# Scores for the maximum in PSUM banks of their own, one job ahead, and one bank for layer matmuls until the last exponential

## What is computed

```python
x_norm = _ln(x, norm1_w) * (1 + sc_msa) + sh_msa
q, k, v = ...                                   # projections, rotary embedding in layer 0
s = jnp.einsum('bqhd,bkhd->bhqk', q, k) * scale
s = jnp.where(mask, s, jnp.finfo(s.dtype).min)
a = jax.nn.softmax(s, axis=-1)
self_out = jnp.einsum('bhqk,bkhd->bqhd', a, v).reshape(b, s, d) @ attn_out_W
x = x + g_msa * self_out
h = jax.nn.gelu(xm @ mlp_W1 + mlp_b1, approximate=True)
x = x + g_mlp * (h @ mlp_W2 + mlp_b2)
```

## Time and profile before

| | us |
|---|---|
| median of 3 executions | 800.41 |
| lowest, highest | 796.43, 803.18 |
| the profiled execution | 800.15 |
| its span, first to last instruction | 798.3 |
| TensorE matmul busy | 648.6 (81%) |
| VectorE busy | 431.4 (54%) |
| ScalarE busy | 419.8 (53%) |
| GpSimd busy | 220.0 (28%) |
| mean granted clock of TensorE | 0.944 |

### The profile page before, as it was taken

The page is one execution under the profiler, slowest core; times in us unless marked ns, Lnnn a source line. Parts: engine busy times, 40 slices in busy tenths (PEclk is TensorE's granted clock), DMA queues, the critical chain, the costliest instruction groups (busy, mean ns, idle before and its releaser), DMA issues.

```text
span 798.3 us, 16559 instructions
## 1 busy us (share of the span) xinstructions
PE 648.6 (81%) x6694; PEld 364.3 (46%) x6732; DVE 431.4 (54%) x1121; ACT 419.8 (53%) x714; POOL 220.0 (28%) x319
## 2 busy tenths in 40 slices
PE   5579887888879987888788878888899788868887
PEld 5234443444444544445345444543456443644445
DVE  2447767646665676566655666666555652231222
ACT  0141634555465464736474457365676639465453
POOL 3142433305341434323431334143131420000000
PEclk9689999998989999999999899999999989989899
DMA  8500000000000000000000000000000000000000
GB/s 302 175 2 1 16 1 15 14 2 28 15 1 2 15 14 15 2 14 15 16 1 2 24 5 2 15 1 15 1 2 14 2 1 2 0 14 1 0 14 13
DMA packets 15314, 15.81 MB, mean 20 GB/s; under 512 B 1833, under 2 KB 13108, under 8 KB 14856
## 3 DMA queue, kind: packets, MB, share of 16 engines
q1 hardware_dynamic: 14572, 10.72, 4.5%
q10 hardware_dynamic: 668, 4.05, 1.3%
HBM read 13.66 MB, written 1.09 MB: 18 GB/s over the span
## 4 chain that ended last, share of the span: by engine, by line
PE 51%; ACT 27%; DVE 15%; issue 4%; POOL 1%; DMA 1%; SPq 0%; DVEq 0%; ACTq 0%; POOLq 0%
ACT P L576 13%; PE lin L938 12%; PE lin L951 9%; PE big L1027 8%; PE avp L1055 6%; DVE mhl L773 5%; PE big L1006 3%; ACT hT L559 3%; ACT xn L548 2%; PE big L1034 2%; DVE bst L725 2%; PE big L1022 2%; ACT hid L610 2%; PE lin L960 2%; DVE oT L805 1%
## 5 line engine op out<-in xcount | busy, mean ns | idle before, releaser
L773 DVE TENSOR_REDUCE mhl<-big 128x8 bf16<-128x616 f32 (+1 forms) x160 | 151.0, 963 | 95.0 <-PE big L1006 92.6
L504 POOL TENSOR_TENSOR qm<-qT,hm 128x512 f32<-128x512 f32 x80 | 88.0, 1100 | 125.8 <-ACT qT L541 77.3
L938 PE MATMUL lin<-hT,W 128*128 128x512 f32 x184 | 107.7, 673 | 14.5 <-ACT hid L610 6.1
L576 ACT ACTIVATE P<-big,padcol 128x1024 f32<-128x1024 f32 x64 | 67.9, 1114 | 73.0 <-PE big L1034 73.0
L576 ACT ACTIVATE P<-big 128x1024 f32<-128x1024 f32 x64 | 62.0, 1021 | 78.0 <-PE big L1034 77.9
L1027 PE MATMUL big<-qm,kT 32*128 32x512 f32 x640 | 99.7, 695 | 0.0
L467 POOL TENSOR_SCALAR rstd<-mv 128x4 f32<-128x4 f32 (+1 forms) x36 | 8.4, 233 | 313.7 <-DVE mv L731 313.5
L1055 PE MATMUL avp<-P,Vp 128*32 128x128 f32 x2560 | 91.0, 285 | 1.3 <-DVE Vp L740 1.2
L490 POOL TENSOR_TENSOR kbm<-kT,hm 128x308 bf16<-128x308 f32 (+1 forms) x80 | 68.2, 853 | 58.0 <-PE big L1006 47.9
L1055 PEld LDWEIGHTS avp<-P,Vp 128*32 128x32 f32 x2560 | 68.2, 113 | 29.0 <-issue 24.5
L1006 PE MATMUL big<-kbm,qb 32*128 32x308 bf16 (+1 forms) x320 | 54.6, 342 | 29.0 <-ACT P L576 27.5
(11 more groups left out here) (160 smaller groups left out, 929.7 us busy)
## 6 DMA issues: line engine op xcount, KB each, us to landing
gring<-gate_rows SPq DMA_DIRECT2D x20, 256.0 KB, 3.5
W<-in_w ACTq DMA_DIRECT2D x2, 1152.0 KB, 12.3
hid<-in_ws SPq DMA_DIRECT2D x2, 832.0 KB, 5.5
W<-in_w ACTq DMA_DIRECT2D x1, 1088.0 KB, 7.3
x<-in_x SPq DMA_DIRECT2D x4, 256.0 KB, 9.9
out<-x SPq DMA_DIRECT2D x4, 256.0 KB, 2.0
ctx<-in_ctx SPq DMA_DIRECT2D x4, 154.0 KB
ctxT<-in_ctxT SPq DMA_DIRECT2D x4, 154.0 KB
```

Source lines behind the costliest of these rows:

```text
L504: nc.gpsimd.tensor_tensor(qm[:, j % 2], q.broadcast_to([128, 4, T]), mask.broadcast_to([128, 4, T]), ALU.mult).then_inc(qm_ready, 1)
L576: nc.scalar.activation(P[:, 8 * half:8 * half + 8, :], big[:, 2 * half:2 * half + 2, :].rearrange("p g (h q) -> p (g h) q", h=4), ACT.Exp, ...
L773: v.tensor_reduce(mhl[:].rearrange("p (g c) -> p g c", c=32)[:, 2 * half:2 * half + 2, 0:4], big[:, 2 * half:2 * half + 2, 0:4 * kw].rearr ...
L938: i = mm(lin_ap(st, s, job, m)[:, 0:n], w, a, start=(c == 0), stop=(c == len(parts) - 1))
```

## The change

- PSUM: `lin` has one bank before `END` instead of two, and after `END` the four banks of `big` are layer banks too, in turn with it (five). `mtp` is no bank of its own any more but a part of `avp`'s. Scores for the maximum have two banks `sc`, used by both halves of a job in turn.
- TensorE's order: slot 0 has the values product of the job before, the turn, the first half of the next job's scores, and the transposed scores. The subtraction is in slot 1, behind the layer units of slot 0. The second half of the next scores is in slot 2. Slot 3 has layer units only.
- The scores for the maximum wait for the reduction of the half before them, not for exponentials. The transposed scores wait for the exponentials of the job before, which the values product waits for too.
- VectorE: maxima in slots 0 and 2; the division is cut in two parts, slots 0 and 1. ScalarE: exponentials in slot 1.
- `keep_warm` and `IDLE` are gone.
- The layer units' slots are moved: chains end 8 slots ahead of their block instead of 6 and begin 2 later; three tails begin 2 later.
- VectorE's setup sets `rden` once for each of five `lin_free` semaphores.

```diff
@@ -33,6 +33,9 @@
 NC = GB * C
 HALF = T // 2
+NQ = 2
+GQ = 4 // NQ
+NLIN = 1
 BIG = 2.0 ** 100
 SCALE = float(HD) ** -0.5
@@ -128,16 +131,16 @@
 ]
-TAILS = [(16 * 14, 16 * 18), (16 * 17, END + 16), (16 * 19, END + 60), (END + 16, END + 76)]
+TAILS = [(16 * 14 + 2, 16 * 18), (16 * 17 + 2, END + 16), (16 * 19 + 2, END + 60), (END + 16, END + 76)]
...
     if k == NAT:
         return TAILS[s]
-    end = 16 * POS[k, s] - 6
+    end = 16 * POS[k, s] - 8
     if k:
-        return 16 * (POS[k - 1, s] + 1), end
+        return 16 * (POS[k - 1, s] + 1) + 2, end
     return max(16 * POS[k, s] - 28, 0), end
@@ -170,24 +173,27 @@
     UNITS.append(("A", _slot // 4, _slot % 4))
     UNITS += [("B", u, s) for slot, u, s in PLACED if slot == _slot]
-IDLE = [j for j in range(JOBS) if not any(slot == 4 * j and u[1] not in ("stat", "apply") for slot, u, s in PLACED)]
 UNITS += [("END", None, None)] + [("B", u, s) for slot, u, s in PLACED if slot >= END]
-LIN_AT, _n = {}, 0
+LIN_AT, _uses, _ended, _next = {}, [0] * (NLIN + 4), False, 0
 for _kind, _u, _s in UNITS:
+    if _kind == "END":
+        _ended, _next = True, 0
     if _kind == "B" and _u[1] not in ("stat", "apply"):
         for _job in ([_u[1] + "a", _u[1] + "b"] if _u in (("p0", "q"), ("p0", "k")) else [_u[1]]):
-            LIN_AT[(_u[0], _s, _job)] = _n
-            _n += 1
+            _bank = _next % (NLIN + 4 if _ended else NLIN)
+            _uses[_bank] += 1
+            LIN_AT[(_u[0], _s, _job)] = _bank, _uses[_bank]
+            _next += 1
 def lin_bank(st, s, job):
-    return LIN_AT[(st, s, job)] % 2
+    return LIN_AT[(st, s, job)][0]
 def lin_turn(st, s, job):
-    return LIN_AT[(st, s, job)] // 2 + 1
+    return LIN_AT[(st, s, job)][1]
@@ -248,11 +254,11 @@
-        lin = ps("lin", [128, 2, 512])
+        lin = ps("lin", [128, NLIN, 512])
         big = ps("big", [128, 4, 512])
         avp = ps("avp", [128, 512])
-        mtpf = ps("mtp", [128, 512])
-        mtp = mtpf[:].bitcast(BF16)
+        sc = ps("sc", [128, GQ, 512])
+        mtp = avp[:].bitcast(BF16)[:, 4 * T:5 * T]
@@ -347,8 +353,8 @@
         rows_done, rows_in = sem("rows_done"), sem("rows_in")
         bias_mm = sem("bias_mm")
-        lin_full = [sem(f"lin_full{i}") for i in range(2)]
-        lin_free = [sem(f"lin_free{i}") for i in range(2)]
+        lin_full = [sem(f"lin_full{i}") for i in range(NLIN + 4)]
+        lin_free = [sem(f"lin_free{i}") for i in range(NLIN + 4)]
         ln_bn, ln_stats, ln_eps, ln_pow, ln_rstd, ln_xn = ([sem(f"{n}{s}") for s in range(NS)] for n in (
             "ln_bn", "ln_stats", "ln_eps", "ln_pow", "ln_rstd", "ln_xn"))
@@ -387,7 +393,8 @@
         def lin_ap(st, s, job, p=128):
-            return lin[0:p, lin_bank(st, s, job), :]
+            i = lin_bank(st, s, job)
+            return lin[0:p, i, :] if i < NLIN else big[0:p, i - NLIN, :]
         def diag(s, kw):
@@ -485,7 +492,7 @@
                 if j >= 2:
-                    pool.wait_ge(s_full, job_turn(j - 2, 1, 2))
+                    pool.wait_ge(s_full, job_turn(j - 2, NQ - 1, NQ))
                 k = kT[s][:, b * kw:(b + 1) * kw].unsqueeze(1)
                 nc.gpsimd.tensor_tensor(kbm[:, j % 2, :, 0:kw], k.broadcast_to([128, 4, kw]),
@@ -621,7 +628,7 @@
                 if kind == "START":
                     act.wait_ge(gate_rows_out, 16)
-                elif kind == "A" and s == 0:
+                elif kind == "A" and s == 1:
                     exps(u, 0)
                     exps(u, 1)
@@ -651,9 +658,10 @@
-            v.memset(rowb[:], 0.0).then_inc(lin_free[0], 1)
+            v.memset(rowb[:], 0.0)
+            for i, free in enumerate(lin_free):
+                v.memset(rden[:, i, :], 0.0).then_inc(free, 1)
             chain(v.memset(mcb[:], 0.0))
-            v.memset(rden[:], 0.0).then_inc(lin_free[1], 1)
             v.memset(oneb[:], 1.0)
             chain(v.memset(mhl[:], 0.0))
@@ -766,26 +774,30 @@
                     v.tensor_copy(qb[s][:], qT[s][:]).then_inc(qb_ready, 1)
-            def maxima(j, half):
+            def maxima(j, part):
                 kw = ATT[job_of(j)[0]]["kw"]
-                dve.wait_ge(s_full, job_turn(j, half, 2))
-                v.tensor_reduce(mhl[:].rearrange("p (g c) -> p g c", c=32)[:, 2 * half:2 * half + 2, 0:4],
-                                big[:, 2 * half:2 * half + 2, 0:4 * kw].rearrange("p g (h k) -> p g h k", h=4), AX,
+                dve.wait_ge(s_full, job_turn(j, part, NQ))
+                v.tensor_reduce(mhl[:].rearrange("p (g c) -> p g c", c=32)[:, GQ * part:GQ * part + GQ, 0:4],
+                                sc[:, :, 0:4 * kw].rearrange("p g (h k) -> p g h k", h=4), AX,
                                 ALU.max).then_inc(m_ready, 1)
             def turned(j):
                 dve.wait_ge(mt_full, job_turn(j))
-                v.tensor_copy(mT[:], mtp[:, 0:T]).then_inc(mt_ready, 1)
+                v.tensor_copy(mT[:], mtp).then_inc(mt_ready, 1)
             def normalise(j):
-                _, s, b = job_of(j)
                 n = job_turn(j)
                 dve.wait_ge(av_full, n)
...
                 v.reciprocal(rden[:], avT[:].rearrange("p k (h d) -> p k h d", d=8)[:, :, 2:4, 0]).then_inc(rden_ready, 1)
+
+            def normalised(j):
+
+                _, s, b = job_of(j)
+                n = job_turn(j)
                 dve.wait_ge(rden_ready, n)
                 v.tensor_tensor(onT[:].rearrange("p (k h d) -> p k h d", h=2, d=8),
@@ -872,17 +884,20 @@
             for kind, u, s in UNITS:
                 if kind == "START":
-                    for half in range(2):
-                        maxima(0, half)
+                    for part in range(NQ):
+                        maxima(0, part)
                 elif kind == "A":
                     if s == 0:
                         turned(u)
-                        if u > 0:
-                            normalise(u - 1)
-                    elif s < 3 and u + 1 < JOBS:
-                        maxima(u + 1, s - 1)
+                    if u + 1 < JOBS and s % GQ == 0:
+                        maxima(u + 1, s // GQ)
+                    if u > 0 and s == 0:
+                        normalise(u - 1)
+                    if u > 0 and s == 1:
+                        normalised(u - 1)
                 elif kind == "END":
                     normalise(JOBS - 1)
+                    normalised(JOBS - 1)
                 elif kind == "B":
                     st, part = u
@@ -983,40 +998,42 @@
                     tokens(st, s, "v", [kv], [W[:, VBLK[a], :]], t=A["kw"])
-            def scores(j, half):
+            def scores(j, part):
                 a, s, b = job_of(j)
                 kw = ATT[a]["kw"]
-                if half == 0:
+                if part == 0:
                     if b == 0:
                         pe.wait_ge(qb_ready, QB_ORDER.index((a, s)) + 1)
                     pe.wait_ge(kbm_ready, job_turn(j))
-                pe.wait_ge(st_free, job_turn(j, half, 2))
-                for g in (2 * half, 2 * half + 1):
-                    o = big[:, g, 0:4 * kw].rearrange("p (h k) -> p h k", h=4)
+                if j + part > 0:
+                    pe.wait_ge(m_ready, NQ * j + part)
+                groups = range(GQ * part, GQ * part + GQ)
+                for g in groups:
+                    o = sc[:, g % GQ, 0:4 * kw].rearrange("p (h k) -> p h k", h=4)
                     if a == 0:
                         mm(o, identb[:], mqk[:].unsqueeze(1).broadcast_to([128, 4, T]), start=True, stop=False)
...
                         mm(o, oneb[:, 0:T], mcb[:, (s * GB + b) * C:(s * GB + b + 1) * C].unsqueeze(1).broadcast_to([128, 4, C]),
                            start=True, stop=False)
-                for g in (2 * half, 2 * half + 1):
+                for g in groups:
                     r = slice(32 * g, 32 * g + 32)
-                    o = big[:, g, 0:4 * kw].rearrange("p (h k) -> p h k", h=4)
+                    o = sc[:, g % GQ, 0:4 * kw].rearrange("p (h k) -> p h k", h=4)
                     i = mm(o, qb[s][r, b * T:(b + 1) * T], kbm[r, j % 2, :, 0:kw], start=(a > 1), stop=True)
                 i.then_inc(s_full, 1)
             def turn(j):
-                pe.wait_ge(m_ready, job_turn(j, 1, 2))
-                nc.tensor.transpose(mtp[:, 0:T], mhl[:], identb[:]).then_inc(mt_full, 1)
+                pe.wait_ge(m_ready, job_turn(j, NQ - 1, NQ))
+                nc.tensor.transpose(mtp, mhl[:], identb[:]).then_inc(mt_full, 1)
             def scores_t(j):
...
                 kw = ATT[a]["kw"]
-                pe.wait_ge(m_ready, job_turn(j, 1, 2))
+                pe.wait_ge(st_free, job_turn(j, 1, 2))
                 if a == 0:
                     for g in range(4):
@@ -1027,6 +1044,8 @@
                        qm[r, j % 2], start=(a > 0), stop=False, skip_group_check=True)
+            def subtract(j):
+
                 pe.wait_ge(mt_ready, job_turn(j))
@@ -1035,11 +1054,6 @@
                             i.then_inc(st_full, 1)
-
```

(23 more changed lines are left out.)

## The result

| | before | after |
|---|---|---|
| median, us (lowest, highest) | 801.79 (796.43 to 807.0) | 912.69 (912.1 to 914.9) |
| span of the profiled execution | 798.3 | 910.3 |
| start, to the first turned maxima | 44.4 | 51.5 |
| attention stretch | 618.7 | 722.0 |
| tail, to the end of the span | 135.2 | 136.8 |

The ratio is 1.139, 95% interval 1.131 to 1.147: 13.9% slower, some 111 us. The prediction was 833 with a range up to 863; it had the sign and missed the size by 80 us. One hundredth of a ratio is 8 us.

A forecast was written before the change was run, and what follows sets the result against it. It took the kernel for a loop of handovers with no engine full. Start 45.6, attention stretch 655 (611 + 24 table loads + 16 clock + 4 waits) and tail 131 gave 831.6 of span, 833 us predicted, range 788 to 863.

The forecast's parts named there:

- The single bank: Attention stretch: each layer unit waits until the unit before is emptied from the one bank; adds 73 us.
- The sign to look for: TensorE's layer matmuls would wait some 60 to 90 us in all for ScalarE and VectorE.
- the 13 of late exponentials: Slot 0 work emptied by ScalarE stands ahead of the exponentials in its queue: 29 jobs, 13 us net.
- table loads: Attention stretch, ScalarE: 19 loads of 1.28 us between exponentials and gelu, silu or sigmoid emptying; 24 us.
- The rest of the sum: Attention stretch without bank terms: 525 us of structure, 24 table loads, 16 clock, 4 remaining VectorE and data waits.
- the warming matmuls at nothing: Three useless matmuls in each of 38 jobs, beside exponentials TensorE waited for: removal saves nothing, may cost clock.
- the clock falls: Rival: without warming matmuls the attention stretch's mean clock drops from 0.95 to 0.85, 33 us more, 866; chance 0.13.
- the gain of the order: Attention stretch: new order gains 18 us by structure, and 30 from maxima no longer holding the turn.
- the 76 us: Old attention stretch, 543 summed against 618.7 measured: put down to clock, VectorE ahead of maxima and data waits.
- The start: Until the first turned maxima: second half of first scores waits for maxima of the first, 1.2 us more, 45.6.
- The tail: Layer work after the last exponential: five banks take 7 us off 135.2, two more units add 2.7; 131.
- Empty jobs: Jobs without layer work: time between turned maxima would be 5.0 to 5.1 us, no gain over 4.97.

The follow-up runs named there:

- version with two banks and narrow halves: Changed kernel, two layer banks before END; both score groups of a half from the same 32 rows into one bank, exponential scale 0: 848.2 us, ratio 1.066.
- the stand-in: Kernel before, with both score groups of a half from the same 32 rows into one bank, read twice, exponential scale 0: 820.6 us, ratio 1.028.

## Why the prediction was wrong, step by step

**The sum and what was measured.** The span was to be 831.6 and was 910.3. The 78.7 us between are 5.9 in the start (51.5 against 45.6), 67 in the attention stretch (722 against 655), 5.8 in the tail (136.8 against 131).

**The single bank: right in kind and in size.** The sign to look for, 60 to 90 us of layer waits, came out at 115.7. For the price, take the bank out of the sum: 655 less 73, and less the 13 of late exponentials, is 569 for the attention stretch. The version with two banks and narrow halves took 660.4 there, and 638 with the 22 of the stand-in off; its profiled execution was 5 us under its median, so 638 to 643. The single bank is then 79 to 84 of the 722.0, where the sum had 86, and 14 more among its table loads (11 of the 19). The Trainium skill, "Perfetto Trace Analysis", section "Matmuls", tells to rotate independent groups through PSUM banks; the trace agrees, and the run with one bank in the old order has a price, 22% of the whole.

**The rest of the sum: what failed.** All but the bank was to take 569 us and took 638 to 643. The sum had the new order some 50 us faster than the 618.7 of before, and by these runs it is 20 to 25 slower. Two steps did that: the warming matmuls put at nothing, and a gain credited to the order.

**The first step that failed: the warming matmuls at nothing.** I took 16 us from the mean clock of 0.95 before and left it as it was, and wrote that the removal of the warming matmuls "saves nothing and may cost clock". In the old order it costs 30 us by itself, in the new order with two banks 17. That TensorE waits for the exponentials there is true; but the matmuls behind such a wait then ran slower: the values product had a mean of 310 ns without the warming matmuls, 285 with them. The sum also had bank waits and clock as separate terms, where the trace has them in one chain: in job 14 a wait of 2.27 us was followed by the lower level, and then a unit took 2.08 plus 0.78 where I had 1.00 plus 0.84. Against the version with two banks, which has the same units in the same jobs, 33 jobs whose granted clock was under 0.9 took 374 us instead of 307, and the other 46 jobs 348 instead of 353, with the price of the stand-in in the times of both groups. So the difference lies in the jobs with the low clock. They hold 88 of 168 layer units and have the long waits too, so this does not tell how much is clock and how much is waiting. The rival "the clock falls" had nearly the right clock (0.85, measured 0.87) and put it at 33 us; with that the forecast would have been 866, still 47 short.

**The second step, and the larger: the gain of the order.** The sum gave the new order 18 us by structure and up to 30 for maxima that no longer hold the turn. More than that, it set the old order at 543 against 618.7 measured, and of the 76 us between, it kept only 16 of clock and 4 of waits for the new one. Without warming on either side the ratio is 1.038 for the new order with two banks and the stand-in off, and 1.038 for the old: no difference. With warming on both sides it is 1.016, 13 us slower with 8 either way. Of the 69 to 74 us that the rest of the sum was short, 17 to 30 are the warming matmuls, and some 40 to 57 are left to this step. The wait for maxima did fall from 21.1 to 6.0 us, but the values product now stands 51.7 us behind the exponentials. Which of the 76 us came back in the new order, and where, no run parts.

**Table loads.** 24 us were charged to the new order beyond what the old one pays; measured 24, with 10 either way. One load took 1.283 us. The Trainium skill, "ScalarE: Activation LUTs", section "What ACT_TABLE_LOAD costs", has about 2.66 us for a switch, of which the load itself is 1.283 as here and the rest a drain. The row of 178.66 to 179.95 us stands directly behind the exponentials and directly ahead of the gelu with no drain between, so here the measurement decides.

**The start.** I added 1.2 us for the wait between the halves, which is there (1.32), and overlooked that the projections ahead of the first scores take the single bank as well: four handovers of 0.78 to 0.85 and matmuls that stayed at 2.08 us a pair.

**The tail.** Five banks were taken at 7 and gave 10.4. It was still 6 us longer than reckoned: TensorE was busy 108.1 us at 0.91, in the old kernel with six banks 101.1 at 0.97, of which 2.7 are the two more units.

**Empty jobs.** I had 5.0 to 5.1 us. Of the seven jobs without layer matmuls, one took 4.6 us and the others 5.6 to 7.0, some with masks, some at a clock of 0.65 to 0.80; the four quickest jobs of all (4.6, 4.8, 5.2 and 5.2) hold one unit or none. So this sign is met only in part.

**Right.** The turn waits nearly vanish. The sign.

So the 111 us are, by ratios: single bank 81, warming matmuls gone and the new order together 30. The last two can't be parted further: the warming is worth 30 in the old order and 17 to 19 in the new, the order the rest. The 81 rest on the stand-in costing the new order what it cost the old. The moved layer units, and `mtp` in the bank of `avp`, were not tried by themselves; they are in what is here called the order.

## What to carry to other kernels

Count the banks of every stream that is woven into the loop before giving one away: a stream with a single bank costs its emptying at each unit, and where the emptying shares a queue with the long work, that work too. Price an idle gap on TensorE twice, once as time and once as what runs slower behind it: with one bank in the old order that was 47 and 33 us in the tail. Useless matmuls in a wait can be worth more than they cost, and to take them out needs a run of its own. And where a sum falls short of the kernel that was measured (here 543 against 618.7), carry what is missing over to the new kernel in full, until a run shows that it goes.

## What was not expected of the hardware

- 114 matmuls of 512 columns into the bank of `mtp`, in waits, are worth 30 us of 800; the clock of the attention stretch is 0.95 with them and 0.89 without.
- In the old order a single bank lengthened the tail from 135 to 215 us, at a clock of 0.79.
- Two matmuls of 32 rows each took 0.30 us together when they came from different rows, and 0.43 from the same; with masks between them, 320 of them kept TensorE busy 93.5 us instead of 54.6.
- The clock column said 1.00 in a start whose matmuls took 2.08 us, the duration of the lower level; only durations told it.
